# First layer of a two-layer transformer: paired heads in the score product, context out of its bank by ScalarE, bias and context lows on GpSimd, weight scales loaded as they are

## The reference, cut to what matters

```python
qkv = xn @ Wqkv.T + b                  # 256 columns of q, 16 of k, 16 of v
scores = einsum('bqhd,bkd->bhqk', q, k) * 16**-0.5   # then the causal mask
ctx = softmax(scores) @ v
x1 = x + (ctx @ out_w.T + out_b) + ffn(xn)
```

## Time and profile before

| | |
|---|---|
| time, median of 3 runs | 1162.2 us (1160.7 to 1166.5) |
| the profiled execution | 1162.8 us, span 1161.0 us |
| busy, share of the span | PE 92%, PEld 85%, DVE 72%, ACT 59%, POOL 41% |
| first layer, steps 0 to 95 | about 39 to 403 us |

### The profile page before, as it was taken

The page is one execution under the profiler, slowest core; times in us unless marked ns, Lnnn a source line. Parts: engine busy times, 40 slices in busy tenths (PEclk is TensorE's granted clock), DMA queues, the critical chain, the costliest instruction groups (busy, mean ns, idle before and its releaser), DMA issues.

```text
span 1161.0 us, 21474 instructions
## 1 busy us (share of the span) xinstructions
PE 1071.3 (92%) x7506; PEld 982.7 (85%) x7506; DVE 831.8 (72%) x1611; ACT 689.0 (59%) x1916; POOL 480.6 (41%) x544
## 2 busy tenths in 40 slices
PE   4778899989988688999999999999999999999997
PEld 3667788878877677888999999999999999899996
DVE  4677777777775565888777777677777767777775
ACT  3666665666565443555566666666766666555553
POOL 2564554456375100002774434444433434488200
PEclk9899999999999899999999999999999999999999
DMA  7846656664855337662544455454445443233220
GB/s 235 147 146 157 160 169 148 167 206 128 176 180 153 128 104 200 181 221 87 191 128 139 122 168 155 130 151 139 133 133 170 144 131 113 87 108 108 66 98 19
DMA packets 143113, 166.16 MB, mean 143 GB/s; under 512 B 10807, under 2 KB 109112, under 8 KB 142944
## 3 DMA queue, kind: packets, MB, share of 16 engines
q1 hardware_dynamic: 139935, 156.41, 46.8%
q0 software_dynamic: 3072, 8.39, 2.2%
HBM read 116.13 MB, written 48.63 MB: 142 GB/s over the span
## 4 chain that ended last, share of the span: by engine, by line
PE 57%; DVE 11%; DMA 11%; POOL 8%; ACT 5%; SPq 4%; issue 3%; DVEq 0%; POOLq 0%; ACTq 0%
PE ps_m L1644 24%; PE ps_s L1644 10%; DMA scales<-d_scales 7%; PE ps_t L1644 6%; PE ps_b L1644 3%; POOL d_xs L1293 3%; PE ps_c L1644 2%; ACT probs L476 2%; PE ps_t L1760 2%; PE ps_c L1760 2%; PE ps_m L824 2%; SPq L322 1%; DVE neg_max L761 1%; PE ps_b L824 1%; POOL parts L441 1%
## 5 line engine op out<-in xcount | busy, mean ns | idle before, releaser
L1405 ACT ACTIVATE probs_a<-ps_s,neg_max_a 128x256 f32<-128x256 f32 x256 | 118.0, 473 | 144.1 <-DVE neg_max_a L1610 144.1
L1644 PE MATMUL ps_m<-xTa,w_qk 128*128 128x512 f32 x768 | 199.0, 398 | 4.0 <-DVE v L1463 1.6
L1644 PEld LDWEIGHTS ps_m<-xTa,w_qk 128*128 128x128 f32 x768 | 136.9, 188 | 34.2 <-issue 5.4
L476 ACT ACTIVATE probs<-ps_s,neg_max 128x128 f32<-128x128 f32 (+1 forms) x256 | 104.9, 420 | 70.7 <-DVE neg_max L761 69.3
L1610 DVE TENSOR_REDUCE neg_max_a<-ps_s 128x2 f32<-128x512 f32 x128 | 88.1, 691 | 51.9 <-PE ps_s L1644 50.2
L1306 POOL CAST we_down<-raw_down_e 88x512 fp32r<-88x512 f32 x47 | 28.6, 609 | 217.9 <-DMA raw_down_e<-in_we_down 217.9
L1644 PE MATMUL ps_m<-w_v,xTa 128*128 128x256 f32 x768 | 106.2, 288 | 0.0
L1644 PE MATMUL ps_t<-pTa,v 128*128 128x256 f32 x768 | 103.5, 284 | 0.0
L1644 PE MATMUL ps_s<-kTa,qTa 128*128 128x256 f32 x768 | 102.9, 283 | 0.3 <-DVE kTa L1441 0.2
L486 ACT ACTIVATE pT<-ps_t 128x512 fp32r<-128x512 f32 x96 | 57.7, 602 | 67.5 <-PE ps_t L889 66.6
L1644 PEld LDWEIGHTS ps_s<-kTa,qTa 128*128 128x128 f32 x768 | 96.7, 191 | 1.0 <-DVE kTa L1441 0.7
(11 more groups left out here) (248 smaller groups left out, 2783.6 us busy)
## 6 DMA issues: line engine op xcount, KB each, us to landing
w_qk<-d_w_head SPq DMA_DIRECT2D x64, 512.0 KB, 3.9
raw_up<-in_we_up SPq DMA_DIRECT2D x47, 352.0 KB, 3.5
d_w_head<-parts SPq DMA_DIRECT2D x128, 128.0 KB, 2.2
raw_down_e<-in_we_down SPq DMA_DIRECT2D x47, 176.0 KB
codes<-in_w_codes SPq DMA_DIRECT2D x64, 128.0 KB
scales<-d_scales SPq DMA_DIRECT2D x64, 128.0 KB
q<-d_q_scr SPq DMA_DIRECT2D x24, 256.0 KB, 6.7
d_xs<-zeros SPq DMA_DIRECT2D x16, 384.0 KB, 7.7
```

What stands on the lines that cost most here:

```text
L476: last = act.activation(probs[:, g % 3, a * w:(a + 1) * w], ps_s[g % 2][:, a * w:(a + 1) * w], ACT.Exp, bias=neg_max[:, g % 2, a:a + 1], s ...
L1405: last = act.activation(probs[:, s, t, :], ps_s[s][:, t * SEQ:(t + 1) * SEQ], ACT.Exp, bias=neg_max[:, s, t:t + 1], scale=1.0, accum_out=s ...
L1644: last = pe.matmul(out, lhs[i], rhs[j], start=start and n == 0, stop=stop and n == 2, skip_group_check=True)
```

## The change

- **Scores.** Two heads share one product. `q3` is now 2 x (32 rows of q, twice): rows 0 to 63 hold eight heads and rows 64 to 127 the other eight; `k3` holds k for the first group with zeros in rows 64 to 127, and beside it k for the second group with zeros in rows 0 to 63. One product gives the scores of a head of each group, in 256 or 512 columns. The q columns of the weights are put in another order on the way in. k is written by two operations on ScalarE and two on VectorE.
- **Loads of q.** Two DMAs for a sequence in place of three, one for each group. Each writes 64 partitions, 8 KB to a partition, from 32 rows in DRAM that are read twice.
- **Context.** ScalarE copies the bank out (`ctx_raw`), and TensorE's next tile waits for this copy alone. VectorE multiplies `ctx_raw` by the turned reciprocals straight from their bank. GpSimd makes the low part.
- **Bias.** GpSimd adds it to `x_in` after the normalisation has read it, at step 5 of turns 1 to 3; the two products go.
- **x1** has two buffers, and waits for the store of two turns ago.
- **Scales.** No preparation: the chunks' scales are loaded from the input, and for the first 16 chunks GpSimd multiplies them by 128**-0.5 before the split. The first two chunks are loaded in the start-up, ahead of the late weights.
- The memsets of `q3`'s zero rows go.

```diff
         def load_q(p, s):
             sp.wait_ge(q_out[s], 16 * DC * (p + 1))
             if p:
                 sp.wait_ge(s_full.sem, s_full.at(0, (p - 1) * NU + (s + 1) * NU // 2))
-            for r, i in enumerate((0, 1, 0)):
-                sp.dma_start(q3[HD0 * r:HD0 * (r + 1), :, s * SEQ:(s + 1) * SEQ].bitcast(F32),
-                             dram["q_scr"][i, :, s * SEQ:(s + 1) * SEQ].rearrange("(h d) t -> d h t", d=HD0)).then_inc(q3_got[s], 16)
+            for c in range(DC):
+                sp.dma_start(q3[c * P // DC:(c + 1) * P // DC, s].bitcast(F32).rearrange("p j t -> p (j t)"),
+                             dram["q_scr"][s, c].rearrange("i (d j) t -> (i d) (j t)", d=HD0).unsqueeze(0)
+                             .to_broadcast([2, 2 * HD0, HEADS0 // DC * SEQ])).then_inc(q3_got[s], 16)
...
-        sp.dma_start(block_scales[:], dram["w_scales"].rearrange("m a b n -> (m a b) n")).then_inc(scales_in, 16)
+        sp.dma_start(ob[:], dram["out_b"].partition_broadcast(P)).then_inc(ob_in, 16)
+        for n in range(2):
+            load_chunk(n)
...
-        sp.wait_ge(scaled, 1)
-        sp.dma_start(dram["scales"].rearrange("m a b n -> (m a b) n"), block_scales[:]).then_inc(scales_out, 16)
-        sp.wait_ge(scales_out, 16)
-        for n in range(2):
-            load_chunk(n)
...
         def split(n):
...
+            if n < CHUNKS:
+                pool.tensor_scalar(scales[:, b, :], scales[:, b, :], HD1 ** -0.5, None, ALU.mult).then_inc(scaled, 1)
+                pool.wait_ge(scaled, n + 1)
...
+        def output_bias(p):
+
+            pool.wait_ge(ln_done, TP * (p + 1))
+            pool.tensor_tensor(x_in[:, p % 2], x_in[:, p % 2], ob[:].unsqueeze(1).to_broadcast([P, TP, D]), ALU.add).then_inc(biased, 1)
+
+        def context_low(p, i):
+            pool.wait_ge(ctx_high.sem, ctx_high.at(0, TP * p + i + 1))
+            pool.tensor_tensor(cT[1][:, i, :, :].rearrange("p c n -> p (c n)"), ctx_f[:],
+                               cT[0][:, i, :, :].rearrange("p c n -> p (c n)").bitcast(F32), ALU.subtract).then_inc(ctx_low.sem, 1)
+
         pool.sem_inc(h_low.sem, 2)
         inverse_root(0, TP)
+        pool.wait_ge(ob_in, 16)
+        output_bias(0)
+        split(0)
         lows(front)
-        for n in range(2):
-            split(n)
+        split(1)
         for g in range(END):
             p, n = divmod(g, NU)
+            if n == BIAS_AT and 0 < p < TURNS:
+                output_bias(p)
             if g in ln_stats_at:
                 inverse_root(ln_stats_at[g][1] * TP // 2, TP // 2)
             for kind, _, i in late[g - 1] if g else ():
                 if kind == "out":
                     inverse_root(stats_of(i), 1)
+            if g in ctx_high_at:
+                context_low(*ctx_high_at[g])
...
+            if g in ctx_at:
+                _, p, i = ctx_at[g]
+                act.wait_ge(pv_ok.sem, pv_ok.at(0, p * NU + group_end[i] + 1))
+                if p or i:
+                    act.wait_ge(item_done.sem, item_done.at(0, number[ctx_before(p, i)] + 1))
+                act.activation(ctx_raw[:], ps_c[:, 0:D], ACT.Copy).then_inc(item_act.sem, 1)
...
-            dve.tensor_tensor(ctx_f[:], ps_c[:, 0:D], rinv_t[:], ALU.mult).then_inc(item_done.sem, 1)
+            dve.tensor_tensor(ctx_f[:], bank(item)[:, 0:D], ctx_raw[:], ALU.mult).then_inc(item_done.sem, 1)
...
             if i == 0:
-                dve.wait_ge(x1_out.sem, x1_out.at(p, 0))
-            dve.tensor_tensor(x1[:, i, :], x_in[:, p % 2, i, :], both_f[:], ALU.add).then_inc(x1_ok.sem, 1)
+                dve.wait_ge(biased, p + 1)
+                if p >= 2:
+                    dve.wait_ge(x1_out.sem, x1_out.at(p - 1, 0))
+            dve.tensor_tensor(x1[p % 2][:, i, :], x_in[:, p % 2, i, :], both_f[:], ALU.add).then_inc(x1_ok.sem, 1)
...
-            for a, h in enumerate(heads):
-                last = pe.matmul(out[:, a * w:(a + 1) * w], q3[:, h, (2 * s + t) * P:(2 * s + t + 1) * P],
-                                 k3[:, s, 0:w], start=False, stop=(a == nh - 1), skip_group_check=True)
+            for a in range(nj):
+                last = pe.matmul(out[:, a * DC * w:(a + 1) * DC * w].rearrange("p (c k) -> p c k", c=DC),
+                                 q3[:, s, j + a, t * P:(t + 1) * P], k3[:, s, :, 0:w],
+                                 start=False, stop=(a == nj - 1), skip_group_check=True)
...
-                pe.matmul(out[:, 0:D], ones_r[:], ob[0][:], start=True, stop=False, skip_group_check=True)
-                pe.matmul(out[:, 0:D], ones_r[:], ob[1][:], start=False, stop=False, skip_group_check=True)
```

More of the change, by code:

```diff
@@ L114, in stage_layer0 @@
     w_o = [sb(f"w_o{i}", [P, DC, D], R32) for i in range(2)]
-    ones_r = sb("ones_r", [1, P], R32)
-    ob = [sb(f"ob{i}", [1, D], R32) for i in range(2)]
+    ob = sb("ob", [P, D])
     w_down = sb("w_down", [P, len(HT), D], R32)
@@ L119, in stage_layer0 @@
     small = sb("small", [P, SMALL])
-    bq, bk = small[:, 0:DC], small[0:48, DC:DC + 1]
+    bq, bk = small[:, 0:DC], small[:, DC:DC + 1]
     s_gate, s_up = (small[:, DC + 1 + i * len(HT):DC + 1 + (i + 1) * len(HT)] for i in range(2))
@@ L235, in chunk_of, with ctx_before @@
         return None if n % 3 == 2 else n // 3 * 2 + n % 3
+    BIAS_AT = 5
+    def ctx_before(p, i):
+        return ("ctx", p, i - 1) if i else ("ctx", p - 1, TP - 1)
     def bank(item):
@@ L310, in load_chunk @@
             sp.dma_start(codes[:, n % 2, :], dram["w_codes"][m, half, :, at:at + PC]).then_inc(w_in[n % 2].sem, 16)
-            sp.dma_start(scales[:, n % 2, :], dram["scales"][m, half, :, at:at + PC].unsqueeze(1).to_broadcast([P // BLOCK, BLOCK, PC]))\
+            sp.dma_start(scales[:, n % 2, :], dram["w_scales"][m, half, :, at:at + PC].unsqueeze(1).to_broadcast([P // BLOCK, BLOCK, PC]))\
                 .then_inc(w_in[n % 2].sem, 16)
@@ L421, in gpsimd @@
                            pattern=[[-1, P]], channel_multiplier=1).then_inc(const_ok, 1)
-        for padded in (k3[:], v_wide[:], q3[:, Q_ZERO[1]:, :]):
+        for padded in (k3[:], v_wide[:]):
             pool.memset(padded.bitcast(F32), 0.0).then_inc(pads_zero, 1)
@@ L531, in early_item @@
             if kind == "kv":
-                high_of(item, k3[0:48, i, :], bank(item)[0:48, 0:SEQ], bk)
+                act.wait_ge(item_full.sem, item_full.at(0, number[item] + 1))
+                act.activation(k3[0:P // DC, i, 0, :], bank(item)[0:P // DC, 0:SEQ], ACT.Identity, bias=bk[0:P // DC])
+                act.activation(k3[P // DC:P, i, 1, :], bank(item)[P // DC:P, 0:SEQ], ACT.Identity, bias=bk[P // DC:P])\
+                    .then_inc(item_act.sem, 1)
             if kind == "ffn":
                 ffn_parts(item)
-            if kind == "ctx":
-                high_of(item, rinv_t[:], bank(item)[:, 0:D])
-        act.wait_ge(zero_ok, 1)
-        act.activation(q3[:, 0:Q_ZERO[0], :].rearrange("p h (a n) -> p (h a) n", n=D),
-                       zeros[:].unsqueeze(1).to_broadcast([P, Q_ZERO[0] * PAIR // D, D]), ACT.Copy)
         act.wait_ge(qkv_in, 32)
@@ L685, in keys_values @@
             dve.wait_ge(item_act.sem, item_act.at(0, act_number[item] + 1))
-            dve.scalar_tensor_tensor(out=k3[32:48, s, :], in0=out[32:48, 0:SEQ], scalar=small[32:48, DC:DC + 1],
-                                     in1=k3[32:48, s, :].bitcast(F32), op0=ALU.add, op1=ALU.subtract)
+            for c in range(DC):
+                low_rows = slice(c * P // DC + 2 * HD0, (c + 1) * P // DC)
+                dve.scalar_tensor_tensor(out=k3[low_rows, s, c, :], in0=out[low_rows, 0:SEQ], scalar=bk[low_rows],
+                                         in1=k3[low_rows, s, c, :].bitcast(F32), op0=ALU.add, op1=ALU.subtract)
             by_part = out[:, SEQ:SEQ + 4 * HD0].rearrange("p (t i d) -> p i t d", t=2, i=2)
@@ L895, in context @@
             if j == 0 and (p or s or t):
-                before = ("ctx", p, 2 * s + t - 1) if s or t else ("ctx", p - 1, TP - 1)
-                pe.wait_ge(item_done.sem, item_done.at(0, number[before] + 1))
+                pe.wait_ge(item_act.sem, item_act.at(0, act_number[ctx_before(p, 2 * s + t)] + 1))
             for a in range(nj):
@@ L965, in item_work @@
             if kind == "out":
-                pe.matmul(out[:, 0:D], ones_r[:], ob[0][:], start=True, stop=False, skip_group_check=True)
-                pe.matmul(out[:, 0:D], ones_r[:], ob[1][:], start=False, stop=False, skip_group_check=True)
                 for c in range(DC):
-                    product3(out[:, 0:D], [x[:, i, c, :] for x in cT], [w[:, c, :] for w in w_o], False, False)
+                    product3(out[:, 0:D], [x[:, i, c, :] for x in cT], [w[:, c, :] for w in w_o], c == 0, False)
                 for m in range(len(HT)):
@@ L1853, in program @@
         ("x1", [TURNS, P, TP * D], F32),
-        ("scales", [4, DC, P // BLOCK, FEAT], F32),
         ("w_head", [4, HEADS1, P, W_HEAD], F32),
```

69 lines of the change are left out of this document (29 added, 40 removed).

## The result

The changed kernel takes 1303.4 us (median; 1301.6 to 1314.5 in 4 runs) against 1161.5 beside it: a ratio of 1.123, 95% interval 1.118 to 1.128. The forecast was 1270, slower. The first rows are from the page of the changed kernel: its busy times, the granted clock in 40 slices, and the chain that ended last.

What follows compares the result with a forecast made beforehand. Middle turns were taken as near TensorE's time, seams as paced by the chunk-load loop. Start-up and first turn +21, three seams +96, less 8 (x1) and 5 (TensorE), plus 4 (clock): net +108, forecast 1270 us, range 1170 to 1315 (own 1225 to 1315).

Steps and rivals of the forecast that it cites:

- Two engines carry a q load: Loads of q: an outermost dimension of 2 puts both DMAs of a half on the same two DMA engines.
- Rival 1: Loads of q spread over all engines, the broadcast being flattened on its way: about 1142 us; chance 0.12.
- Rival 2: Two engines per q DMA, but the two DMAs on different pairs; a load lands in 13.5 us: 1185 us; chance 0.10.
- 24 us a load: Each half of q: 22 us of transfer (18 to 25) plus 2.2 fixed, where it was 9.6 before.
- Seams: Between turns, late q and the chunk loads queued behind it delay rstd: +32 us each, three are +96.
- +21: Start-up and first turn: us lost as q lands late and chunks 2 to 7 wait, delaying the rstd of step 11.
- these low parts: Context lows moved to GpSimd, 0.74 us each: cost 0 beside its waiting, 12 us in all without such cover.
- Start-up 6.3 us sooner: Start-up: no scale preparation moves everything up 7.7 us, writing k in two halves costs 1.4.
- x1: 8 us: Last turn: two x1 buffers remove VectorE's wait for the store of x1, saving 8 us (5.3 to 5.3 + 3.5).
- pairing and bias products: 5 us: TensorE: paired scores save 5 us, dropped bias products 3.8 more; 5 taken, between 0 and 9.
- rival 3: Loads as in rival 1, but GpSimd is the bound and eats 15 to 20 of the gain: 1160 us; chance 0.04.
- Clock: About eight long waits of TensorE drop its clock: 0 to 28 us, taken 4.

Runs made afterwards that it cites:

- e2_pad: e1_spread's four plain q loads with the q scratch padded so that each load's outermost dimension is 2, no broadcast: 1302.5 us, ratio 1.091 to the kernel before.
- g1_spread2: Repeat on another chip of the changed kernel with each half of q loaded in four plain DMAs of 32 rows: 1146.7 us, ratio 0.987 to the kernel before.
- e4_actq: Changed kernel with its broadcast q loads issued by ScalarE on its own queue instead of SyncE's: 1311.5 us, ratio 1.099 to the kernel before.
- e1_spread: Changed kernel with each half of q loaded in four plain DMAs of 32 rows, not two broadcast ones: 1178.6 us, ratio 0.988 to the kernel before.

## Why the prediction was right, and where it was off

The direction and the cause were right; the time was 33 us low, inside the range.

1. *Two engines carry a q load.* Right: share 0.13 with both DMAs of a half in flight, and spread loads take all of the loss away. Rival 1 (1142) is what the kernel becomes when the loads are spread on purpose (1146.7). Rival 2, two pairs of engines, falls: two pairs would give a share of 0.25, and the two DMAs of a half land one after the other, at 43 and 54.5 us in the start-up.
2. *24 us a load.* This is the term that was mis-sized: 27.9 to 31.0 for the first halves. The rate taken was 22 GB/s an engine; it was 16.5 at first, when half of the packets or more took 0.6 us, and 26.5 later, when they took 0.31. The forecast allowed 18 to 25 us for the transfer, so 20 to 27 with its fixed 2.2. Of its signs, two missed by this: the first half was to be there before 50 us and came at 54.5, and TensorE was to stand about 10 us at each turn's first step and stood 17 to 25. With loads of 23 to 25 us (e2_pad) the loss was 125 us, and the forecast's sum for 24 us stood 128 above its sum for spread loads (1270 and 1142). So the structure of the sum held, and the load's duration, by the step from e2_pad to the changed kernel, makes 34.5 of the 37 us by which +108 missed the +144.8 at step 95.
3. *Seams.* +32 was forecast for each. With loads of 23 to 25 the turns' first steps in e2_pad are at 148.6, 273.7 and 398.8, and the last step at 513.1, where g1_spread2 has 105.0, 201.9, 293.3 and 387.7: 15 us in the start-up, 28, 28 and 34 up to the next turns' starts and 20 in the last. Those cuts go through the seams. Between them the distance of the two kernels hardly moves, and read there (from step 15 of a turn on) it is 27.8 us in the first turn, then 60.0, 91.7 and 122: seams of 32, 32 and 30, for loads of about the forecast length, against the +32. The first turn's 27.8 answers to the forecast's +21 and the 6.3 us by which the kernel with spread loads starts sooner. In the changed kernel, with its longer loads, the same distance is 35.0, then 77.0, 118.1 and 160: 42 a seam. The way it goes was right: first q's arrival at the turn's first step, then rstd behind the chunk of steps 5 to 7 (VectorE 57.2 us). At the last seam it was not rstd that TensorE waited for but a context low part, which stood in GpSimd's queue behind a split that waited 25.74 us for its chunk. The forecast had put these low parts at nothing, because they follow a step in which GpSimd is waiting anyway; that wait is just what they stand behind. They took the place of rstd there, and what they added was not tried by itself:

```profile
474.19 0.72 POOL L438 TENSOR_TENSOR parts<-codes,scales 128x256 fp32r<-128x256 f32 x1 [25.74 <-DMA scales<-in_w_scales]
...
476.47 0.72 POOL L460 TENSOR_TENSOR cT<-ctx_f,cT 128x256 fp32r<-128x256 f32 x1
...
477.24 1.65 PE L842 MATMUL ps_m<-w_o,cT 128*128 128x256 f32 x6 [26.51 <-POOL cT L460]
```

   What the forecast did not name either is SyncE itself standing at the issue of the next DMA (13.7 us for two stores, 23.1 for one load of x at 26.86). The match of the sum suggests that this changed the order of the waiting more than its sum. That was not tried, and without q loads in SyncE's queue (e4_actq) 27 us came back.
4. *Start-up 6.3 us sooner.* Right: with spread loads the first step starts at 33.0 (e1_spread) and 32.3 (g1_spread2), against 39.4.
5. *x1: 8 us; pairing and bias products: 5 us.* Too high. The last turn shows 4 to 5 us for x1, and pairing nothing that can be told; the bias products were not tried by themselves. The whole gain up to step 95 in e1_spread is 15.1 us where the forecast had 20.
6. *GpSimd.* The bias addition was 2.36 us, as worked out (2.4). The scale multiplication, 0.85, was not within its bounds (0.3 to 0.75): one input, and yet slower than two (0.72 to 0.74 in the rows above).

```profile
L436 POOL TENSOR_SCALAR scales<-scales x16: 848/849/931, 14.7 to 168.4; 128x256 f32<-128x256 f32 x16
...
L456 POOL TENSOR_TENSOR x_in<-x_in,ob x4: 2337/2357/2401, 11.0 to 479.4; 128x1024 f32<-128x1024 f32 x4
```

   (Both rows give minimum, median and maximum in ns.) Of rival 3, the cost that GpSimd adds is there, but 9 us and not 15 to 20, and it doesn't reach the gains.
7. *Clock.* The mean granted clock in the four turns is 0.79 to 0.87, where it was 0.95 to 1.00 before. While TensorE waits for q in the start-up it is 0.50 (the windows from 34 on, above), and the work behind a long wait begins at half, as here just after q's arrival at 294.3, with TensorE busy throughout:

```profile
296.00:298.00 2.00, 2.00 (x11) 2.00 (x11) 0.98 (x2) 1.55 (x8) 0.32 (x1) 0.50 0.25 83
```

   TensorE is busy 336.7 us in the first layer of the changed kernel and 325.1 in g1_spread2's with the same instructions, so the lower clock makes its work 12 us longer, partly beside other waits; 4 were taken, within 0 to 28.

## What to carry to other kernels

Before a DMA is changed, read the outermost dimension of both sides: gathering a transfer into fewer, bigger DMAs with a small outermost dimension can put it on two engines of sixteen, and what comes behind it waits there too, even from another queue (133 of 160 us stayed). Write a broadcast as several plain DMAs, or lay the source out so that a multiple of 16 is outermost; here that turned 12% slower into 1.3% faster, and with the scales' load as well into 2.4%. A load's duration in a loop without slack counts once in full: with the q loads in SyncE's queue the loss followed it about one to one, from 7 to 30 us a load. And work that is moved to an engine that waits anyway is not free for that: it cost 9 us here, although GpSimd stood 69.5 us for scales.

## What was not expected of the hardware

- SyncE's issue of a later DMA took up to 23.1 us (before, two stores behind a q load took 1.3 together), and up to 12 us also when the slow load was in another engine's queue (e4_actq). From SyncE's timeline of the changed kernel:

```profile
24.45 2.37 SPq L343 DMA_DIRECT2D q<-d_q_scr  x4
26.86 23.12 SPq L328 DMA_DIRECT2D x_in<-in_x  x1
```

- Two engines that carry the two copies of one broadcast moved 33 GB/s for 16 us, in the first DMA of a half, and 53 after that, in the second; with different rows 53 to 55 throughout. Why is open.
- GpSimd's multiplication by a constant over 128x256 took 0.85 us, its product of two tensors of that shape 0.72 to 0.74.
